# Softmax attention stage: maximum's parts written from GpSimd's queue, and Silu as x / (1 + exp(-x)) on three engines

## What is computed

```python
xn = layer_norm(x, norm_w, norm_b)
q = (xn @ q_w + q_b).reshape(B, T, H, -1)          # H = 16 heads of 16 columns
k = (xn @ k_w + k_b).reshape(B, T, H, -1)
att = einsum('bnhl,bmhl->bnmh', q, k) + (1.0 - mask) * -1000000.0
att = softmax(att, axis=2)
v = ((xn @ v_w + v_b) * src_mask).reshape(B, T, H, -1)
y = einsum('bnmh,bmhl->bnhl', att, v).reshape(B, T, D)
scale, shift = split(silu(emb) @ emb_w + emb_b)
h = layer_norm(y, sb_norm_w, sb_norm_b) * (1.0 + scale) + shift
out = x + silu(h) @ out_w + out_b
```

## Time and profile before

| | us |
|---|---|
| median of 3 runs | 3138.68 (3132.44 to 3150.77) |
| the profiled execution | 3141.71 |
| its span in the trace | 3140.0 |
| TensorE busy | 2479.9 |
| ScalarE busy | 2210.1 |
| VectorE busy | 2199.4 |
| GpSimd busy | 1787.2 |

### The profile page before, as it was taken

One profiled execution on the slowest core, in us unless ns is written; L12 is line 12 of the kernel. 1 busy time (PEld: TensorE's weight loads), 2 busy tenths in 40 slices (PEclk: granted clock), 3 DMA queues, 4 the chain that ended last, 5 costly groups with the idle time before them and its releaser, 6 DMA issues. The chain is left out here.

```text
span 3140.0 us, 43803 instructions
## 1 busy us (share of the span) xinstructions
PE 2479.9 (79%) x14276; PEld 1685.0 (54%) x14276; DVE 2199.4 (70%) x2822; ACT 2210.1 (70%) x3641; POOL 1787.2 (57%) x1413
## 2 busy tenths in 40 slices
PE   7787478888888888638898998848877778877885
PEld 4555256667667667512333333225665666656674
DVE  4443379778779788556776777428888778788883
ACT  2333499898898999514665666638987888878992
POOL 0000289879878889640111111027888878888895
PEclk9989699999989999867998999969999999999997
DMA  3000211101111011154555544021112112111111
GB/s 110 27 27 21 72 35 56 56 35 64 51 40 63 35 50 56 53 98 49 82 82 83 83 76 76 21 72 35 51 40 67 60 35 73 41 66 56 48 63 49
DMA packets 106136, 177.18 MB, mean 56 GB/s; under 512 B 10709, under 2 KB 91405, under 8 KB 97199
## 3 DMA queue, kind: packets, MB, share of 16 engines
q1 hardware_dynamic: 101679, 161.69, 20.0%
q0 software_dynamic: 4224, 12.59, 1.3%
HBM read 139.70 MB, written 34.14 MB: 55 GB/s over the span
## 5 line engine op out<-in xcount | busy, mean ns | idle before, releaser
L1068 POOL TENSOR_TENSOR l_h<-l_h,l_c_all 128x512 f32<-128x512 f32 x1024 | 1380.7, 1366 | 267.0 <-DVE l_h L990 251.0
L990 DVE TENSOR_TENSOR_SCAN l_h<-l_dA,l_ps_dbu 128x512 f32<-128x512 f32 x1024 | 1212.9, 1209 | 339.5 <-ACT l_dA L880 169.7
L1243 PE MATMUL l_ps_dbu<-ident,l_dub 128*128 128x128 f32 x4096 | 652.1, 284 | 230.6 <-ACT l_dub L866 152.3
L866 ACT ACTIVATE l_dub<-l_duT,l_b_tok 128x512 f32<-128x512 f32 x1024 | 727.4, 715 | 83.3 <-PE l_ps_dbu L1243 75.6
L880 ACT ACTIVATE l_dA<-l_dt,l_a_neg 128x512 f32<-128x512 f32 x1024 | 728.4, 715 | 0.2
L1218 PE MATMUL l_ps_y<-ident,l_h 128*128 128x128 f32 x4096 | 643.2, 281 | 26.8 <-POOL l_h L1068 22.3
L1243 PEld LDWEIGHTS l_ps_dbu<-ident,l_dub 128*128 128x128 f32 x4096 | 487.4, 145 | 288.6 <-DVE l_h L990 150.3
L1218 PEld LDWEIGHTS l_ps_y<-ident,l_h 128*128 128x128 f32 x4096 | 501.8, 146 | 167.3 <-issue 94.5
L1733 ACT ACTIVATE l_probs<-l_ring 128x512 f32<-128x512 f32 x512 | 293.1, 598 | 264.1 <-PE l_ring L1871 262.8
L1552 DVE TENSOR_REDUCE l_q_max<-l_ring 128x1 f32<-128x512 f32 x512 | 338.6, 683 | 177.9 <-PE l_ring L1864 176.8
L1871 PE MATMUL l_ring<-l_qs,l_ks 102*128 102x512 bf16 x512 | 202.3, 399 | 59.9 <-DMA l_qs<-l_m_parts 49.3
(11 more groups left out here) (246 smaller groups left out, 3056.2 us busy)
## 6 DMA issues: line engine op xcount, KB each, us to landing
l_c_all<-c_rows_dram SPq DMA_DIRECT2D x64, 1024.0 KB, 4.8
l_res<-x_dram SPq DMA_DIRECT2D x24, 512.0 KB, 5.6
parts_dram<-l_parts SPq DMA_DIRECT2D x48, 256.0 KB, 2.9
l_qs<-parts_dram SPq DMA_DIRECT2D x48, 256.0 KB
l_ks<-parts_dram SPq DMA_DIRECT2D x48, 256.0 KB
l_x_in<-x_dram SPq DMA_DIRECT2D x16, 512.0 KB, 5.8
x_dram<-l_res SPq DMA_DIRECT2D x16, 512.0 KB, 2.9
l_x_in<-in_x SPq DMA_DIRECT2D x8, 512.0 KB, 4.2
```

What stands on the lines that cost most here:

```text
L866: return act.activation(dub[:, n % 2, t, :], duT[:, p, t, :], ACT.Copy, scale=b_tok[:, p, t, n:n + 1])
L990: dve.tensor_tensor_scan(h[:, h_slot(s), :], dA[:, s % DA_RING, :], ps_dbu[:, dbu_slot(s), :], 0.0, ALU.mult, ALU.add).then_inc(scan_ok, 1)
L1068: pool.tensor_tensor(h[:, h_slot(s), :], h[:, h_slot(s), :], c_all[:, (n // C_GROUP) % 2, n % C_GROUP, :], ALU.mult).then_inc(hc_ok, 1)
L1243: last = pe.transpose(ps_dbu[:, dbu_slot(s), t * P:(t + 1) * P], dub[:, n % 2, t, j * P:(j + 1) * P], ident[:])
```

## The change

Two things change. The three DMAs of `max_out` leave SyncE's queue and are issued by GpSimd at the end of `max_rest`; SyncE keeps one wait for the parts of group 1 ahead of `stack`. And `silu_half` is taken apart: VectorE computes x = scale * y + shift from PSUM into `hT` (`silu_in`, s = 28 and 29), ScalarE exp(-x) from the same PSUM tile with negated coefficients (`silu_exp`, s = 29 and 30), GpSimd adds 1 (`silu_add`), VectorE takes the reciprocal (`sigmoid`, s = 31 and 32), and GpSimd multiplies (`silu_out`). Exp is in the table that is loaded anyway, so both table loads go. TensorE may reuse the PSUM tiles as soon as the exponential has read them, `project_out` moves to s = 35, 37, 39 and 41, and `result` to s = 38 and 42.

```diff
+        e_neg, neg_coef = sb("e_neg", [P, T]), sb("neg_coef", [P, 2, DH, B])
+        e_half = (e_neg[:], rest[:, 1, :])
...
-                def max_out(b, p, g):
-                    sp.wait_ge(m3_ok, b * GROUPS + g + 1)
-                    for a in range(3):
-                        sp.dma_start(qs[MAX_AT + a:MAX_AT + a + 1, p, g * GH:(g + 1) * GH, :].rearrange("o h (t n) -> o (h t) n", n=P),
-                                     m_parts[:, g, a, :]).then_inc(m_ld[g], 16)
-
...
-                    max_out(b, p, 1)
                     if has_next:
+                        sp.wait_ge(m3_ok, b * GROUPS + 2)
                         stack(b + 1, 1 - p)
-                    max_out(b, p, 2)
...
-                    max_out(b, p, 3)
-                    if has_next:
-                        max_out(b + 1, 1 - p, 0)
...
-                def max_rest(b, g):
+                def max_rest(b, p, g):
...
+                    pool.wait_ge(m3_ok, n)
+                    pool.sem_inc(passed_p, 1)
+                    for a in range(3):
+                        pool.dma_start(qs[MAX_AT + a:MAX_AT + a + 1, p, g * GH:(g + 1) * GH, :].rearrange("o h (t n) -> o (h t) n", n=P),
+                                       m_parts[:, g, a, :]).then_inc(m_ld[g], 16)
+
+                def silu_add(b, h):
+                    pool.wait_ge(e_ok, b * DH + h + 1)
+                    pool.sem_inc(passed_p, 1)
+                    pool.tensor_scalar(e_half[h], e_half[h], 1.0, None, ALU.add).then_inc(e1_ok, 1)
+
+                def silu_out(b, h):
+                    pool.wait_ge(sig_ok, b * DH + h + 1)
+                    pool.sem_inc(passed_p, 1)
+                    pool.tensor_tensor(hT[:, h, :], hT[:, h, :], e_half[h], ALU.mult).then_inc(hT_ok, 1)
...
+                    if has_post:
+                        for h in range(DH):
+                            silu_add(b - 1, h)
+                        for h in range(DH):
+                            silu_out(b - 1, h)
...
+                def silu_in(b, h):
+                    dve.wait_ge(yn_tr, b * DH + h + 1)
+                    dve.tensor_scalar(hT[:, h, :], halves[h][:], coef[:, 2, 0, h, bass.ds(b, 1)], coef[:, 2, 1, h, bass.ds(b, 1)],
+                                      ALU.mult, ALU.add).then_inc(mod_ok, 1)
+
+                def sigmoid(b, h):
+                    dve.wait_ge(e1_ok, b * DH + h + 1)
+                    dve.reciprocal(e_half[h], e_half[h]).then_inc(sig_ok, 1)
...
+                                if s in (28, 29): silu_in(b - 1, s - 28)
+                                if s in (31, 32): sigmoid(b - 1, s - 31)
...
-                            if has_post and s in (36, 39): result(b - 1, (s - 36) // 3)
+                            if has_post and s in (38, 42): result(b - 1, (s - 38) // 4)
...
-                def silu_half(b, h):
-                    act.wait_ge(yn_tr, b * DH + h + 1)
-                    act.activation(hT[:, h, :], halves[h][:], ACT.Silu, scale=coef[:, 2, 0, h, bass.ds(b, 1)],
-                                   bias=coef[:, 2, 1, h, bass.ds(b, 1)]).then_inc(hT_ok, 1)
-                    if h == DH - 1:
-                        act.preload_act_table_set(EXP_LN)
+                def silu_exp(b, h):
+                    if first(b) and h == 0:
+                        act.wait_ge(neg_ok, 1)
+                    act.wait_ge(mod_ok, b * DH + h + 1)
+                    if not first(b):
+                        act.wait_ge(hT_ok, b * DH)
+                    if h:
+                        act.wait_ge(p3_ok, min(b + 3, B) * 2 * DH if isinstance(b, int) else (b + 3) * 2 * DH)
+                    act.activation(e_half[h], halves[h][:], ACT.Exp, scale=neg_coef[:, 0, h, bass.ds(b, 1)], bias=neg_coef[:, 1, h, bass.ds(b, 1)]).then_inc(e_ok, 1)
...
-                    take(halves[h], hT_ok, b * DH + h + 1)
+                    take(halves[h], e_ok, b * DH + h + 1)
...
-                            if has_post and s in (33, 34, 35, 37): project_out(b - 1, (33, 34, 35, 37).index(s))
+                            if has_post and s in (35, 37, 39, 41): project_out(b - 1, (s - 35) // 2)
```

More of the change, by code:

```diff
@@ L1336, in softmax_attention @@
         st_ok, ln_a, ln_b, passed, passed_p = sem("st"), sem("ln_a"), sem("ln_b"), sem("passed"), sem("passed_p")
+        neg_ok, mod_ok, e_ok, e1_ok, sig_ok = sem("neg"), sem("mod"), sem("e"), sem("e1"), sem("sig")
+        e_half = (e_neg[:], rest[:, 1, :])
         OUT = TB // 2
@@ L1440, in _ @@
                 load_x(2)
-                max_out(0, 0, 0)
                 run(sp)
@@ L1475, in max_rest @@
                     pool.tensor_tensor(m_parts[:, g, 2, :], m_rest[:], m_parts[:, g, 1, :], ALU.subtract).then_inc(m3_ok, 1)
+                    pool.wait_ge(m3_ok, n)
[11 more added lines that the diff above has]
+                    pool.tensor_tensor(hT[:, h, :], hT[:, h, :], e_half[h], ALU.mult).then_inc(hT_ok, 1)
                 @batches
                 def run(b, p, has_post, has_next, has_after):
-                    max_rest(b, 1)
-                    max_rest(b, 2)
+                    max_rest(b, p, 1)
+                    max_rest(b, p, 2)
                     if has_after:
                         rest_parts(b + 2, 0, 0)
-                    max_rest(b, 3)
+                    if has_post:
[3 more added lines that the diff above has]
+                            silu_out(b - 1, h)
+                    max_rest(b, p, 3)
                     if has_after:
@@ L1486, in run @@
                     if has_next:
-                        max_rest(b + 1, 0)
+                        max_rest(b + 1, 1 - p, 0)
                     if has_after:
@@ L1495, in _ @@
                             rest_parts(b, i, g)
-                max_rest(0, 0)
+                max_rest(0, 0, 0)
                 run(pool)
+                for h in range(DH):
+                    silu_add(B - 1, h)
+                for h in range(DH):
+                    silu_out(B - 1, h)
             @block.vector
@@ L1501, in _ @@
                 dve.sem_inc(smax_ok, RING)
+                dve.tensor_scalar(neg_coef[:], coef[:, 2, :, :, :], -1.0, None, ALU.mult).then_inc(neg_ok, 1)
                 def ln_stats(b, t2):
@@ L1674, in _ @@
                     ln2_apply(B - 1, t2)
+                for h in range(DH):
+                    silu_in(B - 1, h)
+                for h in range(DH):
+                    sigmoid(B - 1, h)
                 for t in range(OUT):
@@ L1743, in run @@
                             if s in (27, 43, 59): products_out(b, s // (2 * GU) - 1)
-                            if has_post and s == 29:
-                                for h in range(DH):
-                                    silu_half(b - 1, h)
+                            if has_post and s in (29, 30): silu_exp(b - 1, s - 29)
                             if has_after:
@@ L1769, in _ @@
                 for h in range(DH):
-                    silu_half(B - 1, h)
+                    silu_exp(B - 1, h)
             @block.tensor
```

## The result

| | before | after |
|---|---|---|
| median, us | 3138.6 (3132.4 to 3150.8, 4 runs) | 3170.1 (3167.6 to 3173.3, 4 runs) |
| span of the profiled execution | 3140.0 | 3166.2 |

What follows compares the result with a forecast made beforehand. TensorE's stop at s = 32 for the maximum's parts, with the stack's end close behind, was taken as the bound; -2.1 + 2 + 7 + 7 + 10 = +24 us on 3138.7 gave 3163 us, range 3134 to 3186.

Steps and rivals of the forecast that it cites:

- The signs that the prediction named: Reciprocal 3.4 us; 4.6 us stack wait at s = 32; some 4 before first projections; clock 0.50; end about 9 longer.
- The reciprocal: VectorE's 128x512 instruction in the Silu: 3.36 us from the slope of three smaller ones, bounds 0.74 and 4.3 us.
- What bounds the kernel: TensorE's stop at s = 32: behind the wait for the parts stands the stack's, ending at about 1541 to 1544.
- The stack starts and ends 2.0 us earlier: SyncE loses three issues ahead of the stack, which then ends at 1542.6 at the latest; batch 0 gains 2.1 us.
- Batches 1 to 6: Steps with the new Silu chain: +1.2 us a batch, +7 in all; group 3's parts counted separately.
- The chain itself: Batch 1's Silu through VectorE's two reciprocals and GpSimd's product: project_out at s = 35 starts at 1548.5.
- the cheaper of my two cases: Low clock after the first projection in batch 1: ending at 1552.8 as before, +0.1 us; the other, lasting 8.1 us, +2.1.
- Group 2's parts: Small DMAs for s = 32, issued by GpSimd: landed by 1532.4, 1.7 us after issue, hidden by 5 us.
- the parts are as late as before: Rival, chance 0.12: GpSimd's DMAs wait for the stack's packets or issue late, s = 32 starts at 1544.6; +13.5, 3176 us.
- Group 3: Parts for s = 48, with little cover from GpSimd: a new wait of 0 to 0.5 us, up to 1; taken as +2.
- Batch 0: No earlier batch to finish, so only the earlier stack counts: -2.1 us.
- Batch 7 and the end: Last batch's chain without a stack, +7 us; end of the layer, where nothing overlaps the chain, +10 us.

Runs made afterwards that it cites:

- the first edit alone: The kernel before with only the maximum's parts copied by GpSimd's queue, the Silu staying on ScalarE with its table loads: 3134.7 us, ratio 0.9978.

## Why the forecast held, and where it was off

The signs that the prediction named came out so. The reciprocal's mean is 3.35 us, the clock is at 0.50 around the chain, and 9.7 us more lie ahead of the last projections: right. At s = 32 TensorE waits for the parts, 5.7 us in batch 1 and 2.6 to 4.2 in batches 2 to 6, not 4.6 for the stack: wrong. The stop ahead of the first projection is 2.8 to 3.1 us in batches 1 to 6, with 0.6 to 2.0 more for an earlier maximum in three of them, and 7.9 in batch 7, where I had some 4 in each: right in kind.

**What bounds the kernel.** Right: the stack lands at nearly the same time as the parts. In before it is 0.6 us ahead of the last of them in batch 1 (1544.0, where I had 1541 to 1544), in after 1.0 behind (1539.5 and 1538.5), and in the first edit alone 1.03 us more of waiting for it follow the parts.

**"The stack starts and ends 2.0 us earlier".** Wrong in batch 1, the batch that I worked with. SyncE's queue there, beside the earlier trace rows, and the queue's own waits:

```profile
1509.70 2.79 SPq L1392 DMA_DIRECT2D l_qs<-parts_dram  x6
...
SPq L1389 <- DMA parts_dram<-l_parts: 7.3, 5, 2.0
```

1509.70 is 1514.48 in the frame of before, where it was 1514.74: 0.3 us earlier, not 2.0. (Counted from the start of its batch the stack lands 0.3 us later in batch 1, and 0.6 to 2.6 us earlier in batches 0 and 2 to 6.) `stack` first waits until `parts_out`'s stores have landed, and that wait, 0.8 to 2.0 us in five batches (1.6 in batch 1), had been hidden behind the three small issues. The code said so, and I had costed the issues removed without asking what is late next in that queue. With the stack's end at 1539.5, which is 1544.3 in before's frame, instead of 1542.6, the second reciprocal starts at 1545.6 where I had 1543.8, and the projection at 1550.5 where I had 1548.5.

**Batches 1 to 6.** This is the term that was mis-sized: 1.2 us each and 0.3 for group 3, and 2.6 measured. Batch by batch (us; before and after are counted from the start of s = 31):

| batch | more up to s = 31 | s = 32, before and after | first projection, before and after | more from s = 31 on |
|---|---|---|---|---|
| forecast | 0 | 7.9, 5.8 | 9.7, 11.7 | +1.2 (+0.3) |
| 1 | 0.0 | 7.9, 6.6 | 9.7, 13.7 | +2.3 |
| 2 | +0.7 | 7.0, 5.1 | 8.8, 11.9 | +2.2 |
| 3 | +2.0 | 7.3, 4.2 | 9.1, 11.9 | -0.1 |
| 4 | +0.2 | 7.4, 4.6 | 9.2, 11.9 | +1.4 |
| 5 | 0.0 | 7.2, 4.1 | 9.0, 11.7 | +2.4 |
| 6 | +1.7 | 6.5, 3.5 | 8.3, 11.7 | +2.6 |
| sum | +4.5 | | | +10.9 |

The chain itself was right: forecast 11.7 us from s = 31 to the first projection, measured 11.7 to 11.9 in batches 2 to 6. Only in batch 1 did it take 2.0 us more, for the reason above. What was wrong is the other side of the difference. I took batch 1's stop for that of every batch, and it is the longest of the six: before resumes 0.5 to 1.5 us sooner in the others, so the same chain costs more there. And 4.5 us lie ahead of s = 31, where the sum had nothing; TensorE's waits for group 1's parts at s = 16 are 4.2 us in these batches. The low clock was near the cheaper of my two cases: it lasted 3.8 to 6.2 us behind the first projection, where I had 4.3 and 8.1. Batch 3 comes out even because its clock was low for 17.1 us around the stop in before and for 13.7 after.

**Group 2's parts.** I wrote "hidden by 5 us", landed by 1532.4; in that frame they let TensorE go on at 1543.4. The step that failed is the landing of 1.7 us, taken from DMAs that had idle engines. The rival "the parts are as late as before" had the mechanism nearly right: beside the stack the parts take 12 us, though s = 32 begins 1.3 to 3.2 us sooner after s = 31 than in before. Its 13.5 us took the whole delay to 1544.6 for lost, against a stack 2.0 us earlier. But `max_scores` of s = 32 needs the stack anyway, so the parts cost there about what they landed later than it: 1.9 us in batch 3, at most 0.3 in the other five. Group 3, for which I had +2, cost nothing to speak of, and group 1, which I had not costed, is the price of this step: 3.0 us of waiting in batch 0 and 0.3 to 2.2 in batches 2 to 5.

**Batch 0.** -3.0 against -2.1, but by other parts than I gave: 2.9 lost up to s = 16, and 5.9 won back behind it, most of it at s = 32.

**The reciprocal.** Right: 3.36 from the slope of three small rows, 3.35 measured, over 16 times the widest of them.
**Batch 7 and the end.** Right: +6.4 against +7, and 9.7 us more ahead of the projection against the +10 of the whole end.

**The sign** rested on one comparison, which the runs confirm: two reciprocals of 3.35 us on VectorE, on the path, against table loads that were covered by another stop. With 0.8 us in the reciprocal's place, or with its work on ScalarE, the change is neutral.

**Luck.** That the sum came within 7 us owes something to errors that cancel: the late group 1 and the shorter stops of before are 6.3 us more than I had in batches 1 to 6, while batch 0, batch 7, the end and 1.7 us in untouched work ahead of the stage are 3.9 us less.

**Slips in the working.** The chain's terms from 1535.9 on add up to 1539.4, not 1539.1. The 10.3 us behind 1548.5 hold three `times_v`, not the four named; the trace has three and 10.2 us at full clock. And the bounds named for the range, 0.1 to 2.1 a batch and 0 to 7 for group 3, give 3155 to 3174 by themselves, not 3150 to 3178.

## What to carry to other kernels

Ask of each wait that is removed which one ends next, in the engine and in its DMA queue; here three lay over one another (the late stack, the small DMAs, the block of ScalarE work). Moving the small DMAs alone won 7 us; an earlier stack and the small DMAs behind three of its DMAs won 22; with the ScalarE work spread as well, and a few more moves, it was 39. An instruction that replaces a covered cost must be covered itself: look for the engine that has slack at that step, and spread its work over several steps. A small transfer that must be on time should be issued ahead of most of a bulk transfer: another queue beside it helped little here (7 us), and on the same queue it waited for what stood ahead of it.

## What the runs showed of the hardware

- A 4 KB DMA issued on SyncE's queue behind 13 DMAs of up to 256 KB took 12.2 to 16.0 us to land in before; behind six of them 10.2 to 12.5, and behind three 5.2 to 6.6, where it was issued right behind them. Alone it took 1.6 to 1.9.
- From GpSimd's queue beside the 13 it took 10.5 to 13.4 us in the changed kernel, from ScalarE's 7.4 to 12.9, against 1.5 to 3.0 without them. Why another queue doesn't pass the bulk transfer is open.
- A float32 reciprocal of 128x512 took VectorE 3.35 us, four times an arithmetic instruction of that size (0.80 from PSUM). On ScalarE the logarithm and the exponential that replace it took 1.24 us.
- The granted clock fell in a stop of 3.8 us (within 1527 to 1528, in the kernel with three DMAs ahead), and also where TensorE was busy 0.60 of a microsecond (within 1531 to 1532 with exp and ln, within 1753 to 1754 with the work spread), but not in batch 1 of the latter, at 0.46 of one.
